# A six-block decoder kernel: the last block's weights split in advance by Pool, and a row of maxima written by ACT

## What is computed

```python
x = _layernorm(x + _L0_attn_ref(x, ...))          # self attention
x = _layernorm(x + _L0_xattn_ref(x, ctx_512, ...))  # first cross attention: 16 heads of 8, 1601 context tokens and the tokens themselves
x = _layernorm(x + _L0_ffn_ref(x, ...))           # mixture of 8 experts
x = _layernorm(x + _L1_attn_ref(x, ...))          # gated linear recurrence
x = _layernorm(x + _L1_xattn_ref(x, ctx_512, ctx_512, ...))  # second cross attention: one head over 1601 context tokens
x = _layernorm(x + _L1_ffn_ref(x, ...))           # last block
# the second cross attention
q = jnp.einsum('bld,de->ble', query, Wq) + bq
k = jnp.einsum('bld,de->ble', key, Wk) + bk
v = jnp.einsum('bld,de->ble', value, Wv) + bv
attn = jax.nn.softmax(jnp.einsum('bqe,bke->bqk', q, k), axis=-1)
out = jnp.einsum('bqk,bke->bqe', attn, v)
# the last block
h = jax.nn.silu(_tlin(x, w1_w, w1_s)) * _tlin(x, w2_w, w2_s)
h = jax.nn.gelu(_tlin(h, h1_w, h1_s), approximate=False)
h = jax.nn.gelu(_tlin(h, h2_w, h2_s), approximate=False)
return _tlin(h, w3_w, w3_s)
```

## Time and profile before

| | us |
|---|---|
| median of 3 runs | 736.56 |
| lowest and highest | 735.44, 743.9 |
| the profiled execution | 738.48 |
| its span, first to last instruction | 736.7 |
| mean granted clock of PE, share of full | 0.939 |

### The profile page before, as it was taken

How to read it: one execution, slowest core, us unless ns; L and a number is a source line. 1 busy time by engine, 2 the same in 40 slices (tenths; PEclk the granted TensorE clock), 3 DMA queues, 4 the chain that set the end, 5 groups by cost and what they waited for, 6 DMA issues and landing times. The chain is left out here.

```text
span 736.7 us, 13537 instructions
## 1 busy us (share of the span) xinstructions
PE 627.8 (85%) x5184; PEld 343.4 (47%) x5184; DVE 530.2 (72%) x705; ACT 427.7 (58%) x769; POOL 206.8 (28%) x251
## 2 busy tenths in 40 slices
PE   7978899999999999999997568997447789969996
PEld 5644433333333333333333246884123467637884
DVE  5368789999999999999842358996596467746342
ACT  3545478888888888888873224555842022244224
POOL 7217432343343665554300020000000560005000
PEclk9998989999999999999999579999769699989999
DMA  8357575555555435435100357540000400000000
GB/s 198 116 123 225 150 231 179 141 132 123 151 153 153 122 100 105 91 95 99 44 2 0 87 213 319 156 145 0 0 0 1 157 1 1 1 0 0 1 1 28
DMA packets 41084, 70.76 MB, mean 96 GB/s; under 512 B 11332, under 2 KB 30108, under 8 KB 40512
## 3 DMA queue, kind: packets, MB, share of 16 engines
q1 hardware_dynamic: 30128, 33.98, 18.3%
q0 software_dynamic: 10288, 33.71, 14.3%
q10 hardware_dynamic: 608, 2.25, 1.4%
HBM read 44.84 MB, written 24.79 MB: 95 GB/s over the span
## 5 line engine op out<-in xcount | busy, mean ns | idle before, releaser
L908 ACT ACTIVATE prob<-ps 128x512 f32<-128x512 f32 (+2 forms) x480 | 253.3, 582 | 48.9 <-PE ps L703 41.0
L1027 DVE TENSOR_REDUCE pm<-ps 128x2 f32<-128x1024 f32 x192 | 226.2, 1216 | 9.0 <-PE ps L665 7.2
L726 PE MATMUL ps<-prob,vst 128*9 128x256 f32 (+1 forms) x1664 | 130.1, 385 | 10.1 <-ACT o_all L896 10.1
L703 PE MATMUL ps<-qq,kc 50*128 50x256 bf16 (+1 forms) x832 | 133.7, 275 | 0.1
L665 PE MATMUL ps<-kc,qq 48*128 48x512 bf16 x384 | 116.9, 391 | 5.4 <-DVE pm L1027 4.3
L703 PEld LDWEIGHTS ps<-qq,kc 50*128 50x128 bf16 (+1 forms) x832 | 52.0, 96 | 93.7 <-ACT prob L908 69.9
L726 PEld LDWEIGHTS ps<-prob,vst 128*9 128x9 f32 (+1 forms) x1664 | 25.1, 88 | 51.7 <-ACT prob L908 39.1
L1839 ACT ACTIVATE prob<-s 128x512 f32<-128x512 f32 (+1 forms) x28 | 15.9, 567 | 56.7 <-PE s L1771 53.9
L1034 DVE TENSOR_REDUCE nm<-ps 128x4 f32<-128x512 f32 (+1 forms) x32 | 30.7, 958 | 15.3 <-PE ps L653 15.3
L665 PEld LDWEIGHTS ps<-kc,qq 48*128 48x128 bf16 x384 | 33.0, 94 | 16.5 <-DVE pm L1027 10.7
L1705 POOL MEMSET pick<- 128x128 f32 x1 | 0.2, 205 | 134.4 <-SPq L1702 134.4
(11 more groups left out here) (354 smaller groups left out, 1318.4 us busy)
## 6 DMA issues: line engine op xcount, KB each, us to landing
kc<-kc_scr SPq DMA_DIRECT2D x32, 300.2 KB, 4.9
comb_bc<-comb_scr SPq DMA_DIRECT2D x8, 512.0 KB, 4.6
kc_scr<-hi POOLq DMA_DIRECT2D x9, 400.2 KB, 4.1
below<-rden_scr POOLq DMA_DIRECT2D x13, 256.0 KB, 9.0
ctx<-ctx_scr POOLq DMA_DIRECT2D x1, 3204.0 KB, 16.3
raw<-in_wexp POOLq DMA_DIRECT2D x8, 384.0 KB, 3.5
exp_scr<-raw_high POOLq DMA_DIRECT2D x8, 384.0 KB, 5.0
exp_scr<-raw_low POOLq DMA_DIRECT2D x8, 384.0 KB, 6.8
```

Source lines behind the costliest of these rows:

```text
L703: last = pe.matmul(bank[0:p, j * TQ:(j + 1) * TQ], kc[s][rows, j, t * 128:t * 128 + p], qq[s][rows, 0, j, :], start=(j == 0), stop=True, s ...
L726: last = pe.matmul(o_ps[32 * hh:32 * hh + VW, kind * TQ + q0:(kind + 1) * TQ], value[:, hh * VW:(hh + 1) * VW], prob[0:k, (NST * n + t) % ...
L908: act.activation(prob[0:p, g % P_RING, 2 * e:2 * e + 2, q0:TQ], s2[0:p, k % S2_RING, 0:2 * w].rearrange("p (i q) -> p i q", i=2), ACT.Exp, ...
L1027: dve.tensor_reduce(pm[:, m % 2, c, :, jt], banks, AX.X, ALU.max).then_inc(s1_read, 1)
```

## The change

In the first cross attention Pool takes three pieces a step instead of two, from step 7: the twelve slabs of the context, and after them eight pieces of the last block's weights. These are now one array `wffn` of 128 x 5632 in DRAM, cut in 768 columns (the last piece has 256); each is loaded, split and stored to a new DRAM array `ffn_scr`. Pool's work in the second cross attention becomes two loads of the split weights, 5.6 MB together. There, the row of maxima is made 128 rows high by PE's matmul, DVE copies it whole to `shift`, and ACT copies `shift` into a pair's PSUM bank before the scores are added: `pick`, the low part of the row and the first matmul of each pair go. ACT's copy for pair k+2 stands in its order after the exponential of pair k; those for the first two pairs of a batch after the last exponential of the batch before. DVE's `row(b + 1)` moves ahead of the sum of batch b's last pair.

```diff
@@ Pool, first cross attention
+                    FW = a["wffn"].shape[1]
+                    ffn_slabs = [(c0, min(3 * DFF, FW - c0)) for c0 in range(0, FW, 3 * DFF)]
+                    def split_ffn(i):
+                        c0, w = ffn_slabs[i]
+                        k, r = E + len(slabs) + i, i % 2
+                        pool.wait_ge(parts_left[r], 32 * (k // 2))
+                        pool.dma_start(raw[r][:, 0:w], a["wffn"][:, c0:c0 + w]).then_inc(raw_in, 16)
+                        pool.wait_ge(raw_in, 16 * (E + i + 1))
+                        pool.tensor_copy(raw_high[r][:, 0:w], raw[r][:, 0:w]).then_inc(raw_split, 1)
+                        pool.wait_ge(raw_split, 2 * k + 1)
+                        pool.tensor_tensor(raw_low[r][:, 0:w], raw[r][:, 0:w], raw_high[r][:, 0:w], ALU.subtract).then_inc(raw_split, 1)
+                        pool.wait_ge(raw_split, 2 * k + 2)
+                        for part, half in enumerate((raw_high[r], raw_low[r])):
+                            pool.dma_start(ffn_scr[part, :, c0:c0 + w], half[:, 0:w].bitcast(F32)).then_inc(parts_left[r], 16)
...
-                            for i in range(2 * (n + 1 - E), min(2 * (n + 2 - E), len(slabs))):
-                                split_slab(i)
+                            for i in range(3 * (n + 1 - E), min(3 * (n + 2 - E), len(slabs) + len(ffn_slabs))):
+                                if i < len(slabs):
+                                    split_slab(i)
+                                else:
+                                    split_ffn(i - len(slabs))
@@ Pool, second cross attention
-                pool.memset(pick[:].bitcast(F32), 0.0).then_inc(set_up, 1)
...
-                for n in FFN_WEIGHTS:
-                    pool.dma_start(ffn_w[n][:], a[n]).then_inc(ffn_in, 16)
-                pool.wait_ge(ffn_in, 16 * len(FFN_WEIGHTS))
-                for i, n in enumerate(FFN_WEIGHTS):
-                    pool.tensor_copy(high_w[n][:], ffn_w[n][:]).then_inc(split, 1)
-                    pool.wait_ge(split, 2 * i + 1)
-                    pool.tensor_tensor(low_w[n][:], ffn_w[n][:], high_w[n][:], ALU.subtract).then_inc(split, 1)
-                    pool.wait_ge(split, 2 * i + 2)
+                for part in range(2):
+                    pool.dma_start(ffn_parts[part][:].bitcast(F32), ffn_scr[part]).then_inc(ffn_in, 16)
+                pool.wait_ge(ffn_in, 32)
@@ PE, max_row and scores_t
-                        o = fin[0:33, t * 128:(t + 1) * 128]
-                        pe.matmul(o, nm_b[:, n:n + 1].to_broadcast([128, 33]), ident, start=True, stop=False)
+                        o = fin[:, t * 128:(t + 1) * 128]
+                        pe.matmul(o, nm_b[:, n:n + 1].to_broadcast([128, 128]), ident, start=True, stop=False)
...
-                    if k >= 2:
-                        pe.wait_ge(exp_done, k - 1)
+                    pe.wait_ge(filled, k + 1)
                     at = slice(b * TQ, (b + 1) * TQ)
-                    if 2 * p + 1 < NKT:
-                        pe.matmul(s2[:, k % 2, :].rearrange("p (i q) -> p i q", i=2), pick[:],
-                                  shift[:, at].unsqueeze(1).to_broadcast([128, 2, TQ]), start=True, stop=False,
-                                  skip_group_check=True)
...
@@ ACT
+                def shifts(k):
+                    b, p = divmod(k, PAIRS)
+                    m, sides = (128, 2) if 2 * p + 1 < NKT else (KLAST, 1)
+                    act.wait_ge(row_sb, b + 1)
+                    if k < 2:
+                        act.wait_ge(qk_sb, k + 1)
+                    else:
+                        act.wait_ge(exp_done, k - 1)
+                    act.activation(s2[0:m, k % 2, 0:sides * TQ].rearrange("p (i q) -> p i q", i=sides),
+                                   shift[0:m, b % 2, :].unsqueeze(1).to_broadcast([m, sides, TQ]), ACT.Copy).then_inc(filled, 1)
+                shifts(0)
+                shifts(1)
...
                         act.activation(prob[0:m, k % RING].rearrange("p i q -> p (i q)")[:, 0:w], s2[0:m, k % 2, 0:w],
                                        ACT.Exp).then_inc(exp_done, 1)
+                        if p < PAIRS - 2:
+                            shifts(k + 2)
+                    if b + 1 < NB:
+                        for p in range(2):
+                            shifts((b + 1) * PAIRS + p)
@@ DVE
-                    dve.tensor_copy(shift[0:33, at], fin[0:33, 0:TQ]).then_inc(row_high, 1)
-                    dve.wait_ge(row_high, b + 1)
-                    dve.tensor_tensor(shift[32:33, at], fin[32:33, 0:TQ], shift[32:33, at], ALU.subtract).then_inc(row_sb, 1)
+                    dve.tensor_copy(shift[:, b % 2, :], fin[:, 0:TQ]).then_inc(row_sb, 1)
...
                     for p in range(PAIRS):
+                        if b + 1 < NB and p == PAIRS - 1:
+                            row(b + 1)
                         add(b, p)
...
-                    if b + 1 < NB:
-                        row(b + 1)
```

More of the change, by code:

```diff
@@ L500, in normalise @@
                         pool.tensor_tensor(o_all[:, n, 0:TQ], o_all[:, n, 0:TQ], o_all[:, n, TQ:2 * TQ], ALU.add).then_inc(ys, 1)
+                    FW = a["wffn"].shape[1]
[12 more added lines that the diff above has]
+                            pool.dma_start(ffn_scr[part, :, c0:c0 + w], half[:, 0:w].bitcast(F32)).then_inc(parts_left[r], 16)
+                    assert len(slabs) % 2 == 0 and E % 2 == 0
                     split_expert(0)
@@ L517, in _ @@
                     for r in range(2):
-                        pool.wait_ge(parts_left[r], 16 * (E + len(slabs)))
+                        pool.wait_ge(parts_left[r], 16 * (E + len(slabs) + len(ffn_slabs)))
                     pool.wait_ge(later_in, 16 * (len(FOR_BLOCK_3) + 1))
@@ L1655, in _ @@
                 dve_ln(1)
-    high_w, low_w = ({n: keep(f"{part}_{n}", a[n].shape, F32R) for n in FFN_WEIGHTS} for part in ("high", "low"))
+    ffn_parts = [keep(f"ffn_{part}", [128, a["wffn"].shape[1]], F32R) for part in ("high", "low")]
+    high_w, low_w = ({n: view.rearrange("p (k n) -> p k n", k=k) for (n, k, _), view in zip(
+        FFN_WEIGHTS, columns_of(part, [k * w for _, k, w in FFN_WEIGHTS]))} for part in ffn_parts)
     with ExitStack() as st:
@@ L1668, in emit_rest @@
         RING = 4
-        ffn_w = {n: sb(f"w_{n}", a[n].shape) for n in FFN_WEIGHTS}
         wq = later["wq6"]
@@ L1678, in emit_rest @@
         qk_high, qk_low = (sb(f"qk_{part}", [2 * CC, T], F32R) for part in ("high", "low"))
-        shift = sb("shift6", [128, T], F32R)
-        pick = sb("pick6", [128, 128], F32R)
+        shift = sb("shift6", [128, 2, TQ])
         bkq = sb("bkq6", [128, 2 * NB])
@@ L1748, in max_row @@
                         n = 2 * b + t
[L1749 to L1751 removed]
+                        o = fin[:, t * 128:(t + 1) * 128]
+                        pe.matmul(o, nm_b[:, n:n + 1].to_broadcast([128, 128]), ident, start=True, stop=False)
+                        last = pe.matmul(o, col["bk6"].to_broadcast([128, 128]), q[:, n * 128:(n + 1) * 128],
                                          start=False, stop=True)
@@ L1757, in scores_t @@
                     k = b * PAIRS + p
-                    if k >= 2:
-                        pe.wait_ge(exp_done, k - 1)
+                    pe.wait_ge(filled, k + 1)
                     at = slice(b * TQ, (b + 1) * TQ)
-                    if 2 * p + 1 < NKT:
-                        pe.matmul(s2[:, k % 2, :].rearrange("p (i q) -> p i q", i=2), pick[:],
-                                  shift[:, at].unsqueeze(1).to_broadcast([128, 2, TQ]), start=True, stop=False,
-                                  skip_group_check=True)
-                    else:
-                        pe.matmul(s2[0:KLAST, k % 2, 0:TQ], pick[:, 0:KLAST], shift[:, at], start=True, stop=False,
-                                  skip_group_check=True)
                     for t in range(2 * p, min(2 * p + 2, NKT)):
```

27 lines of the change are left out of this document (9 added, 18 removed).

## The result

| | before | after |
|---|---|---|
| median (lowest to highest) | 736.75 us (735.44 to 743.9) | 758.9 us (756.94 to 759.86) |
| profiled execution | 738.48 us, span 736.7 | 756.94 us, span 755.1 |
| mean granted clock of TensorE | 0.939 | 0.916 |

The ratio is 1.0277, 95% interval 1.0208 to 1.0346: slower, by 22.2 us in the medians and 18.4 us in the two profiled spans. The forecast was 763 us, range 747 to 777.

What follows compares the result with a forecast made beforehand. Pool's serial chain of splits, broadcast landing and scaling was taken to bound the first cross attention. 736.6 + 30.2 (chain) + 3 (clock) - 6.6 (second cross attention) = 763.2 us, range 747 to 777.

Steps and rivals of the forecast that it cites:

- the load of the split weights: Second cross attention: new 5.6 MB load, at most 51 us without overlap, landed by 622 before the last exponential, so hidden.
- Rival 1: First cross attention: Pool keeps up, results there at 395.75, only the second half counts: 730 us; chance 7 in 100.
- Rival 3: Second cross attention: ACT's copies hold the pairs back, so the second half gives nothing: 770 us; chance 13 in 100.
- Rival 4: First cross attention: Pool's eight further subtractions block DVE, up to 8 x 1.8 us; taken as 0 to 3 us.
- at balance there, with nothing to spare: First cross attention before the change: Pool's chain of 17.5 to 19.3 us a step against a unit of 18.7 us.
- the lower bound of the steps: First cross attention: with shorter landings and pieces, unit 12 is scaled at 410.0, 14.3 us later than before.
- DVE's wait: First cross attention, last unit: denominators land at 366.8, where DVE took the reciprocals at 358.1: 8.7 us.
- no addition: DVE's 8.7 us for unit 12's denominators adds nothing to PE's wait for Pool, but is a floor under the loss.
- The clock: Tail of the first cross attention: after over 20 us of waiting PE starts at the lower clock, 3 us added.
- the stalls behind Pool: Second cross attention: DVE's small subtractions no longer wait for Pool's, gaining 1.2 and 0.7 us.
- The row: Second cross attention: ACT copies replace PE's pick matmuls, gaining 4.4 us over the batches and 0.3 at the start.
- +30.2: First cross attention: Pool scales unit 12 at 425.9, where PE before stood at its projection at 395.75.

Runs made afterwards that it cites:

- the load-ahead kernel: The changed kernel with each piece's load issued one piece ahead, before Pool works on the piece at hand: 734.3 us, ratio 0.9968; once more 733.0 us, 0.9953.

## Why the prediction was right, and where it was not

**Right.** The direction, the mechanism and the place: Pool's chain, three pieces a step, `denominators_out(12)` at 354.4 (362.2 forecast), PE idle at `project(12)` (15.7 us, over 20 forecast), a DVE wait at unit 12's reciprocal, middle stages unchanged, batches near 14.2 us (14.75). The two halves add up as the sum had them, and the load of the split weights is hidden: its parts land after 9.7 and 15.8 us (51 us was the bound). Rival 1 fell: Pool did not keep up. Rival 3 fell: the row of maxima gives 4.0 us, with Pool's splits beside it and without. Rival 4 fell too: with all of Pool's subtractions in the first cross attention, the load-ahead kernel's stage is only 0.2 and 0.8 us longer than before.

**Pool's steps.** The last scaling was to end at 425.9 and ended at 416.2. By steps:

| | forecast | measured | error |
|---|---|---|---|
| step 7 ends its splits | 263.2 | 262.35 | -0.9 |
| steps 8 to 10, together | 64.8 | 54.2 | -10.6 |
| step 11 | 33.5 | 37.2 | +3.7 |
| step 12 | 32.0 | 33.4 | +1.4 |
| step 13 | 22.9 | 22.0 | -0.9 |
| step 14 | 9.5 | 7.1 | -2.4 |

The first -0.9 is no error of the sum, but the lead of 1.0 us that this execution had.

The term that failed is the landing in steps 8 to 10, 9.0 us. It was the median of thirteen landings under one condition and I carried it to another: issued 3.5 to 5.3 us behind the start of SP's group, the same load takes 5.8. The statement behind it failed too, "at balance there, with nothing to spare". The kernel before waits 4.1 to 7.0 us for ACT's output in each of steps 8 to 12. Timeline of Pool, before, steps 8 to 10:

```profile
265.72 0.72 POOL L482 DMA_DIRECT2D below<-o_all  x1 [4.12 <-ACT o_all L896]
...
283.93 0.71 POOL L482 DMA_DIRECT2D below<-o_all  x1 [6.42 <-ACT o_all L896]
...
302.83 0.71 POOL L482 DMA_DIRECT2D below<-o_all  x1 [6.49 <-ACT o_all L896]
```

Issued later, the broadcast landed no later, and the third slab went into that wait. So up to step 11 Pool is not late at all, and rival 1's "step 11 begun as early as before, at about 321" is what happened (320.25). It said 402 for the end of that case. Most of the 14 us from there are the pieces: 28.5 us for 22.5 in step 11, 24.7 for 22.5 in step 12, 13.8 for 13.4 in step 13, together +8.6. (The short piece has a slip in the sum: 7.5 less two thirds of 2.6 is 5.8, not 5.9; it changes nothing.) The contention that I overpriced for the broadcasts I left out for the loads: in the earlier trace rows a load lands in 3.1 to 3.9 us, and the one at 333.05, 1.3 us behind SP's start at 331.73, took 8.1. In three other traces (the weights only, SP's loads later, two pieces less) the same load, issued 0.3 to 1.8 us behind SP's start, took 7.1 to 8.6 us; that SP's group is the cause is argued from this, no run moves the load alone. The landings of steps 11 to 14 (6.6, 6.6, 6.2, 5.0 for 9.0, 7.5, 7.5, 7.5) were 7.0 us under the forecast. So -10.6 and -7.0 for the broadcasts stand against +8.6 for the pieces, and only by the luck of that is the end no more than 9.7 us off. It lies between the lower bound of the steps, 410.0, and the forecast.

The Trainium skill (DMA: Bandwidth & Descriptors, Anatomy of one DMA) gives the broadcast 2.6 us, an estimate from its figures; the lowest landing measured after the change is 5.0 us, so the trace still disagrees, and unit 12 was not ready near 392.

**DVE's wait** for the denominators of unit 12 was 3.3 us for 8.7, as they went out at 354.4 and not at 362.2. That it is "no addition" held only because the wait for Pool covered it. It cost PE 5.8 us (4.7 and the lead of 1.0), more than its own length, with the clock at 0.50 behind it.

**The clock** at the tail: 3 us forecast, 2.8 measured.

**The second cross attention.** 6.6 forecast, 5.0 measured. By runs, the stalls behind Pool are worth 1.0 (1.9 forecast) and the row of maxima 4.0 (4.7). The stalls: only part of the 3.70 us subtraction was on the path; batch 0 is still 0.5 us longer than batch 1 without it. The row: a pair without maxima is 1.25 us, not ACT's 1.35, and it is PE's: the pick's 0.34 us leave PE's order, the next one follows the first of a pair after 0.22 us for 0.12, and 0.23 remain. At a change of batches PE waits 0.67 us for ACT's fill, where it waited 0.52 for DVE.

**The sum.** +30.2 became +20.45, +3 became +2.8, -6.6 became -5.0: 18.3 for the 18.4 us of the spans. The medians say 22.2. Of the 3.8 us between the two, 1.7 come from the profiled execution before, which lies that much above its median, and 2.0 from the one after, which is the fastest of its four; 1.0 us of these is the lead at 105 us, the rest has no place in the trace.

## What to carry to other kernels

Before work is moved onto an engine "with idle time", write that engine's order down as a chain with its waits for transfers, and ask which of them lie in series: here 4.65 us of work a piece were free and 3 to 8 us of waiting a piece were not, and one load issued ahead turned 1.028 into 0.995 to 0.997. A landing time is a reading under one phase against the other queues' loads, so price a moved transfer by rows with the same neighbours. Compare stages from a common instruction to a common instruction: here single executions were up to 5.4 us apart before their kernels differed. And look at where an engine waits in the kernel before: a step that already waits for another engine has room for more.

## What the runs showed of the hardware

- A 256 KB broadcast from DRAM lands in 5.4 to 6.8 us ahead of another queue's group of loads and in 7.4 to 10.9 us together with it; over nine units of two kernels it landed 9.9 to 10.8 us after that group's start, issued from 0.5 us ahead of it to 5.3 us behind.
- Behind such a broadcast in the same queue a load of 384 KB was waited for 11.1 us (SP's group running too) and 6.7 us, one of 128 KB 5.8 us; the same pieces without a broadcast right ahead 7.6, 3.8 and 2.8 us.
- After 2.5 us of idle time of PE (and 0.7 us shortly before) in a stretch of full load the granted clock was 0.50 for the next 6 us, and 3.3 us of delay became 5.8.
- A copy of 128x512 float32 from SBUF to PSUM on ACT takes 0.602 us, as the exponential from PSUM to SBUF does (0.597).
